# Half of a five-tap convolution moved from VectorE to GpSimd in the first two of four attention rounds

## What is computed

```python
def lepe_conv(v, w, b):                      # w: (256, 1, 5), depthwise, padding 2
    x = v.transpose(0, 2, 3, 1).reshape(Bb, H * DV, Ss)
    y = jax.lax.conv_general_dilated(x, w, window_strides=(1,), padding=[(2, 2)],
        dimension_numbers=('NCH', 'OIH', 'NCH'), feature_group_count=H * DV)
    y = y + b[None, :, None]
...
o = mala_attn(q, k, v) + lepe_conv(v, lepe_w, lepe_b)
o = o.reshape(Bb, Ss, H * DV) * o_gate
return o @ Wo.T
```

## Time and profile before

| | us |
|---|---|
| median of 3 runs | 863.48 |
| lowest, highest | 859.68, 867.82 |
| the profiled execution | 868.96 |
| its span | 867.1 |
| TensorE busy | 768.8 (89%) |
| VectorE busy | 472.4 (54%) |
| ScalarE busy | 396.7 (46%) |
| GpSimd busy | 411.9 (47%) |
| mean granted TensorE clock, as a share of full speed | 0.955 |

### The profile page before, as it was taken

The page is one execution under the profiler, slowest core; times in us unless marked ns, Lnnn a source line. Parts: engine busy times, 40 slices in busy tenths (PEclk is TensorE's granted clock), DMA queues, the critical chain, the costliest instruction groups (busy, mean ns, idle before and its releaser), DMA issues.

```text
span 867.1 us, 13292 instructions
## 1 busy us (share of the span) xinstructions
PE 768.8 (89%) x4314; PEld 601.9 (69%) x4314; DVE 472.4 (54%) x1207; ACT 396.7 (46%) x943; POOL 411.9 (47%) x420
## 2 busy tenths in 40 slices
PE   5999999989978977678889898979999999999994
PEld 4665576576456545358778788869988989999451
DVE  3667698688578515242434334434444444444898
ACT  5583757744452442015444344534555555656000
POOL 0000001677656666635666656566555656565400
PEclk9979999999989987899999899999999999999997
DMA  9500010242237974436556665556556556559995
GB/s 329 168 1 0 1 50 16 91 163 121 114 136 255 356 290 162 171 108 203 183 189 205 203 219 193 184 178 203 175 195 192 174 182 201 171 169 337 393 410 219
DMA packets 82621, 158.45 MB, mean 183 GB/s; under 512 B 14446, under 2 KB 55539, under 8 KB 82296
## 3 DMA queue, kind: packets, MB, share of 16 engines
q1 hardware_dynamic: 58344, 96.74, 33.8%
q0 software_dynamic: 19968, 56.67, 16.6%
q10 hardware_dynamic: 4240, 4.19, 1.4%
HBM read 88.15 MB, written 73.57 MB: 186 GB/s over the span
## 4 chain that ended last, share of the span: by engine, by line
PE 57%; another core or an unknown queue 12%; ACT 11%; DVE 10%; issue 8%; ACTq 1%; DMA 0%; DVEq 0%
PE ps_wide L1352 11%; PE ps_wide L1367 7%; PE ps_kv L1352 6%; PE ps_wide L1112 4%; PE ps_narrow L1340 4%; ACT arena L917 3%; ACT arena L900 2%; PE ps_wide L1105 2%; PE ps_wide L1278 2%; PE ps_wide L1134 2%; PE ps_wide L988 2%; PE ps_kv L1134 2%; PE ps_kv L1376 2%; PE ps_narrow L1125 1%
## 5 line engine op out<-in xcount | busy, mean ns | idle before, releaser
L561 POOL DMA_INDIRECT expert_rows<-arena,slot_i x192 | 193.8, 1009 | 243.9 <-DVE arena L1669 147.9
L667 POOL DMA_INDIRECT expert_outs<-arena,meta x224 | 217.9, 973 | 158.3 <-DVE arena L1874 108.8
L917 ACT COPY arena<-arena 128x512 f32 x224 | 127.4, 617 | 193.4 <-remote 109.8
L1874 DVE TENSOR_SCALAR arena<-ps_wide,meta 128x256 f32<-128x256 f32 x224 | 97.9, 479 | 169.4 <-remote 106.6
L1352 PE MATMUL ps_wide<-arena 128*128 128x128 f32 x1200 | 155.6, 281 | 16.6 <-issue 11.2
L1352 PEld LDWEIGHTS ps_wide<-arena 128*128 128x128 f32 x1200 | 148.5, 195 | 29.5 <-issue 15.5
L1367 PE MATMUL ps_wide<-arena 128*128 x448 | 118.4, 388 | 1.6 <-issue 1.6
L1367 PEld LDWEIGHTS ps_wide<-arena 128*128 128x128 f32 x448 | 78.3, 195 | 8.7 <-issue 2.4
L1352 PE MATMUL ps_kv<-arena 128*128 128x128 f32 x592 | 75.7, 280 | 6.5 <-issue 4.7
L1352 PEld LDWEIGHTS ps_kv<-arena 128*128 128x128 f32 x592 | 72.9, 194 | 11.6 <-issue 5.4
L1112 PE MATMUL ps_wide<-arena 128*128 128x512 f32 x160 | 72.1, 597 | 3.2 <-DVE arena L1565 3.2
(11 more groups left out here) (237 smaller groups left out, 1046.1 us busy)
## 6 DMA issues: line engine op xcount, KB each, us to landing
arena<-expert_rows SPq DMA_DIRECT2D x224, 160.0 KB, 3.6
arena<-expert_outs SPq DMA_DIRECT2D x48, 512.0 KB, 12.4
arena<-w_experts SPq DMA_DIRECT2D x32, 384.0 KB
expert_rows<-pad_row SPq DMA_DIRECT2D x33, 160.0 KB
expert_outs<-arena,meta POOLq DMA_INDIRECT x224
out<-x ACTq DMA_DIRECT2D x7, 512.0 KB, 10.2
x<-x SPq DMA_DIRECT2D x3, 1024.0 KB, 11.1
h_cols<-arena SPq DMA_DIRECT2D x6, 512.0 KB
```

The lines of the kernel that those rows point to most:

```text
L561: nc.gpsimd.indirect_dma_start(rows, bass.IndirectOffsetOnAxis(ap=slots_i[b % 2][:, t, k:k + 1], axis=0), hrows[b % 2][:, t, :], None, bou ...
L667: nc.gpsimd.indirect_dma_start(outs, bass.IndirectOffsetOnAxis(ap=meta_i[:, j % METAS, 1:2], axis=0), yb[j % OUTS], None, bounds_check=las ...
L917: last = nc.scalar.copy(wgu[:, j % 4:j % 4 + 1, :], wall[:, bass.ds(expert[j], 1), 0:DOWN])
L1874: v.tensor_scalar(yb[j % OUTS], ps_wide[:, 1, p % 2, j % DUO * D:(j % DUO + 1) * D], meta[:, j % METAS, 0:1], None, ALU.mult).then_inc(s_y ...
```

## The change

In rounds 0 and 1 (b < POOL_TAPS = 2) VectorE's `convolve` works on chunk 0 only. GpSimd's list gets, ahead of its first scatter, two calls of `convolve_second_chunk`: wait for ScalarE's tap 0, and then for each of four taps a product into a scratch row `pool_tap` and an addition onto `lepe[:, 1]`, each behind a wait for the one before. `close_o` waits for GpSimd's eighth instruction of the round before it reads lepe. `pool_tap` (128x1024) lies over `hrow_odd`. The semaphores of the tail are shared by part n and part n + 4, and the counts waited for are raised to match.

```diff
+POOL_TAPS = 2
...
+        pool_tap = take(S, overlay=hrow_at)
...
-        s_fin = [sem(f"s_outputs_in{i}") for i in range(PARTS)]
+        s_fin = [sem(f"s_outputs_in{i}") for i in range(FIN)]
...
-        s_fin_pe = [sem(f"s_outputs_in_for_tensor{i}") for i in range(PARTS)]
+        s_fin_pe = [sem(f"s_outputs_in_for_tensor{i}") for i in range(FIN)]
...
+            def convolve_second_chunk(b):
+
+                pool.wait_ge(s_tap, b + 1)
+                for j in range(1, TAPS):
+                    done = 2 * (b * (TAPS - 1) + j)
+                    nc.gpsimd.tensor_scalar(pool_tap, vt[:, C - 1, j:j + S], lw[:, C - 1, j:j + 1], None,
+                                            ALU.mult).then_inc(s_pool_tap, 1)
+                    pool.wait_ge(s_pool_tap, done - 1)
+                    nc.gpsimd.tensor_tensor(lepe[:, C - 1], lepe[:, C - 1], pool_tap, ALU.add).then_inc(s_pool_tap, 1)
+                    pool.wait_ge(s_pool_tap, done)
+
+            pool.wait_ge(s_w, WAIT_W)
+            for b in range(POOL_TAPS):
+                convolve_second_chunk(b)
             for b in range(B - 2):
                 scatter_through_round(b)
...
-                pe.wait_ge(s_fin_pe[n], 16 * len(BY_PE[n]))
+                pe.wait_ge(s_fin_pe[n % FIN], 16 * sum(len(BY_PE[i]) for i in range(n % FIN, n + 1, FIN)))
...
                     for j in taps:
-                        for c in range(C):
+                        for c in range(C - 1 if b < POOL_TAPS else C):
                             last = v.scalar_tensor_tensor(lepe[:, c], vt[:, c, j:j + S], lw[:, c, j:j + 1], lepe[:, c],
                                                           ALU.mult, ALU.add)
...
                         dve.wait_ge(s_conv, b + 1)
+                        if b < POOL_TAPS:
+                            dve.wait_ge(s_pool_tap, 2 * (b + 1) * (TAPS - 1))
...
-                dve.wait_ge(s_fin[n], 16 * len(planes))
+                earlier = sum(len(BY_DVE[i]) for i in range(n % FIN, n, FIN))
+                dve.wait_ge(s_fin[n % FIN], 16 * (earlier + len(planes)))
```

More of the change, by code:

```diff
@@ L321, in adaln_block_kernel @@
         s_tap, s_hrow = sem("s_first_tap"), sem("s_rows_copied")
+        s_pool_tap = sem("s_chunk_tapped_by_pool")
         s_rowt = sem("s_rows_turned")
@@ L523, in load_plane @@
                 first = ORDER[TAIL[n]] * PART * P
-                landed = s_fin_pe[n] if k in BY_PE[n] else s_fin_end if (n, k) == (PARTS - 1, LATEST) else s_fin[n]
+                at = n % FIN
+                landed = s_fin_pe[at] if k in BY_PE[n] else s_fin_end if (n, k) == (PARTS - 1, LATEST) else s_fin[at]
                 sp.dma_start(fin[n % FIN][k], outs[k * T + first:k * T + first + PART * P, :].rearrange(
```

## The result

The changed kernel takes 882.88 us (median of 6 runs, 879.45 to 884.74) against 865.13 for the kernel before (6 runs): +17.75 us, a ratio of 1.020 with a 95% interval of 1.0165 to 1.0236. It is slower, on the side on which the prediction put 0.38, and just above its range.

The account below looks back on a forecast made before the run. The prediction took TensorE, busy 89% of the span, as the bound. Removed taps gave 0 to 0.1 us, GpSimd hindering VectorE cost +4.8 and +3.9; 863.48 + 8.7 = 872 us, range 860 to 882.

Parts of the forecast that it names:

- the side on which the prediction put 0.38: Whole kernel: the chance given to a result slower by more than 1%; within 1% had 0.57, faster 0.05.
- the gain is nothing: VectorE's removed taps in rounds 0 and 1: 9.9 us of work, claimed worth 0 to 0.1 us.
- The walk: Rounds 0 and 1: VectorE and GpSimd take whole turns on SBUF, numerators +4.8 us, softmax +3.9, sum +8.7.
- the lower bound of a round: GpSimd's eight instructions in a round: 9.8 us at least, 13.8 expected, 22.7 at most.
- the low clock: Round 1 behind TensorE's stall: clock as in round 0, 3.1 us more, total 875; shares a chance of 0.15.
- the upper price: GpSimd's instructions at 2.74 us each: about +23 us over both rounds, 886; shares a chance of 0.15.
- the new bound: GpSimd over 4.4 us an instruction, so close_o waits; at 6 us, +13 a round, 889; shares 0.15.
- one case of 0.15: Rounds 0 and 1: upper GpSimd price or low clock, about +12 us and over, with GpSimd as new bound; chance 0.15.

Follow-up runs that it names:

- e1: The kernel before with taps 1 to 4 of the second chunk left out in rounds 0 and 1, no GpSimd work: 791.35 against 790.36 us.
- e6: The changed kernel with GpSimd's taps of a round started behind mask_kv instead of behind tap 0: 880.14 us against 867.34 for the kernel before.
- e8: The kernel before with dead VectorE work ahead of mask_kv in round 0 and softmax in round 1, no GpSimd arithmetic in the rounds: 879.15 against 867.34 us.
- e7: The changed kernel with unread matmuls (8 and 6) in TensorE's two stalls before the numerators: 875.93 us against 867.34 for the kernel before.
- e12: The changed kernel with 4 and 3 unread matmuls in TensorE's two stalls: 795.55 us against 789.85 for the kernel before.
- e11: The kernel before with four unread matmuls ahead of the summed k-v products of round 0: 868.38 against 868.98 us.
- e10: The changed kernel with 8 and 6 unread matmuls in TensorE's stalls, run beside the changed kernel: 875.37 us, against 883.18 changed and 868.98 before.

## Why the prediction was wrong

**Right: the gain is nothing.** Every group of taps had idle time behind it, or ended with TensorE's logits; e1 measures 1.0002. The idle time behind tap 1 grew from 0.80 to 2.00, as said.

**Right in kind: VectorE and GpSimd take turns.** The walk put the numerators of round 0 at +4.8 and softmax at +3.9, 8.7 in all. Measured are +4.05, and +1.8 for softmax with another 0.7 for the numerators behind it: 6.6. Three terms in it were off, and largely cancelled:

- The product, taken at 1.25 us by ScalarE's row of the same product, takes 2.84 alone and up to 3.94. The nearest row in arithmetic was not the nearest in engine. With the addition at 2.35 (2.0 taken) a round lasts 24 us in place of 13.8. It still ends at 62.9 and 134.6, before lepe is read, so close_o waits for nothing.
- A product does not hold VectorE for its whole length, as the walk had it. Beside a product L1610 in round 0 and L1611 in round 1 were lengthened by 0.82 each, and the next rotation ran beside the same product in 0.69. Both end 1.97 us after their product began; less their own 0.69 that is a hold over the product's first 1.3 us only (an estimate from these rows). An addition holds to its end: L1611 in round 0 (+2.06), L1589 (+0.65) and L1610 at 116.08 (+0.66) all end 0.54 or 0.55 us after one.
- mask_kv was not in the list of what can be held up, because it has one SBUF tensor. L1705 lost 2.14 us beside an addition, on the path, and 0.75 in round 1.

Two slips in the working changed nothing: the lower bound of a round, 9.8 us, leaves out the eight waits of 0.1 (10.6 with them), and the rows used for GpSimd's price lie between 1.2 and 2.7 us for 1024 elements, not between 0.1 and 1.

The sentence from the Trainium skill about exclusion ("SBUF — State Buffer", section "Who interferes with whom") decided the right way, though "the whole instruction" is too much for the products seen here. The Trainium skill's "GPSIMD Engine Reference", section 3, led to an estimate of 2.25 us for the addition; e6 has 2.35. Section 4.1 of that page of the Trainium skill calls one-input work of GpSimd roughly line rate; the product of this kernel is slower than the addition, 2.84 us alone for 1024 elements, and the measurement decides.

**Wrong: what the stall costs.** The step that failed is the low clock. The prediction saw the pattern and worked out 3.1 us for round 1, but held it as a rival beside the forecast, with the upper price and the new bound in one case of 0.15. It is no alternative: in round 1 it comes with the very stall that the forecast itself puts there. And round 1 lost 6.6 us by it, since not the denominators alone but numerators, ranks and broadcast ran at 0.50, and the stretch in round 0 grew by 2.0 more. Added to the walk's 8.7, these 8.7 would have given +17.4, 882.5 on 865.1, beside the measured 882.88; so close it is by luck too (see what stays open). e8 shows the clock without GpSimd, e7 and e12 GpSimd's interference without the low clock.

**What stays open.** The mark and the medians don't go together to better than some 5 us: e12 has +0.6 at the mark and +5.7 in the median, e8 +15.6 and +11.8, e1 -5.3 and +1.0. Part of that may be that round 0 of before has the low clock in some executions only; only one trace of before was read, and its runs on one chip reach from 859.57 to 872.45. Part must be made up or lost behind the mark, which I did not take apart. What brings on the low clock isn't settled either: besides the long stretches behind the stalls there are short ones of 3 to 4 us (e1 and e11 in round 1, behind 0.40 us of idle time; e10 at 138.5, where TensorE had no gap listed since 116), and round 0 of before has its 13.6 us with no more than 1.7 us of idle time ahead of it. Why a product holds VectorE in its first 1.3 us only I can't say; no run separates its reading from the rest.

## What to carry to other kernels

Moving elementwise work from VectorE to GpSimd can take nothing off VectorE's path, or lengthen it, if GpSimd reads SBUF meanwhile: look, before pricing the move, at which VectorE instructions run beside it with two SBUF tensors (or a tensor_scalar from SBUF to SBUF) and who waits for them. An instruction behind which VectorE stands idle anyway was worth nothing here (e1). And when a forecast puts a stall of some 3 or 4 us on a busy TensorE, look at whether a low granted clock follows such gaps elsewhere in the trace, and put it into the sum itself; here it cost more than the stalls.

## What the runs showed of the hardware that was not expected

- GpSimd's product of 128x1024 (one tensor, one weight for each partition) takes 2.84 us alone, its addition of two tensors 2.34 to 2.35, a memset of 128x2560 2.23.
- A VectorE tensor_scalar of 128x8 waits for a whole GpSimd memset (2.29 and 2.25 us in place of 0.16), while a tensor_tensor with both inputs in SBUF beside the same memsets keeps its 0.69.
- GpSimd's product held a VectorE instruction with two SBUF tensors over about its first 1.3 us, its addition to the end (L1610 and L1611 of the changed kernel).
- TensorE stalls of 2.8 to 4.0 us went with 13 to 20 us of a granted clock of 0.50 (in round 0 it fell 1.1 us into the stall, and before has 13.6 us of it there with no idle time over 1.7 us); filling them with work that nobody reads kept it at 1.00 in e7 and e12, and took 7 to 10 us off the changed kernel's median.
